# Transposing the normalised rows on TensorE through PSUM in place of eight DMA transposes, with later due times, in a fused attention and FFN layer

## The chip, the cores and the metric

The kernel runs on all 8 cores of one Trainium2 chip, as one program, each core with two of the 16 sequences. The cores exchange nothing. The time is that of the slowest core, in microseconds (us) on the device. A core has TensorE (PE, matmuls; PEld is its weight load), VectorE (DVE), ScalarE (ACT), GpSimd (POOL) and SyncE (SP); the last two issue the DMAs here. Each engine works through its own instructions in order and waits on semaphores.

## What is computed

The input is x [16, 4096, 1024] in f32. One layer, in two halves, with a LayerNorm before and after each half and a residual around it:

```python
def attn(x, Wq, bq, Wk, bk, Wv, bv, Wo, bo):
    q, k, v = (einsum('bsd,kd->bsk', x, W) + b for W, b in ((Wq, bq), (Wk, bk), (Wv, bv)))
    scores = einsum('bqk,bsk->bqs', q, k) / sqrt(1024)
    sign = where(sign(scores) == 0, 1, sign(scores))
    weights = softmax(where(causal, scores * sign, -inf), axis=2)     # scores * sign = abs(scores)
    return einsum('bqv,dv->bqd', einsum('bqs,bsv->bqv', weights, v), Wo) + bo

def ffn(x, kernel, bias, a, b):        # kernel is first rounded to 4-bit steps
    return einsum('bsd,df->bsf', x, int4(kernel)) + bias + (x @ a) @ b     # rank 16

x = x + layernorm(attn(layernorm(x)))
x = x + layernorm(ffn(layernorm(x)))
```

## The kernel before

**Stages.** A prologue quantises and transposes the weights (until about 330 us). Then each of the two sequences goes through phase A (LayerNorm, Q, K and V projections; Q and K go to DRAM scratch, V stays in SBUF) and phase B (attention, output projection, FFN). Phase B lies at about 811 to 2611 us and 3126 to 4941 us of the profiled execution. A barrier stands between the phases. The change touches phase B alone.

**Phase B.** A sequence has 16 strips of 256 queries; strip s has two tiles of 128 rows (qc = 0, 1) and nt = 2s + 2 flash steps, one for each 128 keys up to the diagonal: nt = 2, 4, ... 32. A flash step j issues, in this order: a load of K (L856, on POOL), emit_S (L794: 8 matmuls 128x256 into SBp; ScalarE's Abs to Sa, L802, and Exp to PT, L815; a mask add on VectorE in the last two steps) and emit_PV of step j - 1 (L835: 8 matmuls into OTp, and two of one column for the row sums, L847). SBp, Sa and PT have two slots. PV(j) waits for Exp(j), and S(j) for Abs(j - 2).

**The epilogue, interleaved.** What follows the attention of a strip is not done at once, but as a list of closures with due fractions. `pre` (L575, L583) evicts OTp right at the start of the next strip. `main` (L738 to L748) has both tiles' output projections and all the rest of tile 0; it is popped during the next strip. `spill` (L749 to L757) has the rest of tile 1 and goes one strip later still. In each strip the pending list is the older spill followed by the newer main, and it is popped strictly in order:

```python
while popped < n_pend and int(pend[popped][0] * nt) <= j:
    pend[popped][1]()
    popped += 1
```

So an entry behind a later due time waits for it: the output projections (0.40 and on) come only once store_stage(1) (0.65) has been popped. What is left after the last strip runs without any flash step beside it: the tile spilled by strip 14 and both tiles of strip 15.

**The closures.** outproj_h (L601: 8 matmuls 128x512 into EB; L609 evicts to t1 on ScalarE). lnattn_a (L623 adds bo, then emit_ln into sqb). lnattn_b (L637 adds x into x2, then emit_ln into lnb, bf16). ln2t_dma (L654). xa_stage (L666: lnT against a_bf into EB, L673 copies to xaT). ffn_h (L683, L689, L692 into EB; L697 evicts to t2). lnffn_chain (emit_ln into sqb, L714 adds the residual into xb). store_stage (the store of y on POOL, and on SP the load of x for the tile four further on). EB is a single PSUM bank of 128x512 f32, shared by outproj_h, xa_stage and ffn_h.

**emit_ln** (L174) is one chain over two engines: VectorE's sum (L188) and sum of squares (L191, which writes sqb), L194; ScalarE's L195, L197, L199, L202; VectorE's L204; ScalarE's scaled write (L207). VectorE, ScalarE and POOL instructions are chained in order, so a ScalarE instruction that waits for VectorE holds all later ones, the flash steps' Abs and Exp too.

**ln2t_dma(qc)** issues eight DMA transposes of 128x128 bf16 on SP, from lnb to lnT, each waiting for the LayerNorm's write. xa_stage waits for all eight.

Of the kernel before, what the change touches and what calls it, by code (L numbers as in the profile page):

```python
# [9 lines left out]
AF = mybir.ActivationFunctionType  # L10
# [21 lines left out]
class Builder:  # L32
# [23 lines left out]
    def dma(self, eng, sem, fn, waits=()):  # L56
        sem.n += 16
        self.queue_sems[eng][sem] = True
        self.ops[eng].append(
            (fn, tuple((s.h, int(v)) for s, v in waits if v > 0), ((sem.h, 16),)))  # L60
        return sem.n


def build_nc(debug=False):
# [29 lines left out]
    with ExitStack() as ctx:  # L94
# [59 lines left out]
        E, dma = B.E, B.dma  # L154
# [382 lines left out]
        def phase_b(seq, EB):  # L537
            wl_val = 0
            for rg, src in ((0, wT_scr["wo"]), (1, wfq_h)):
# [14 lines left out]
                "dv_sqb": {0: (DV, 0), 1: (DV, 0)},  # L554
                "ts_done": {0: 0, 1: 0},
                "pe_ffn": {0: 0, 1: 0},
# [12 lines left out]
            def make_epilogue(s):  # L569
# [49 lines left out]
                def lnattn_a(qc):  # L619
                    def f():  # L620
# [5 lines left out]
                                                waits_src=[(DV, dvb)],  # L626
                                                waits_sq=[st["dv_sqb"][qc]])
                        st["dv_t1"][qc] = dv1
# [3 lines left out]
                def lnattn_b(qc):  # L632
                    def f():
# [6 lines left out]
                            waits=[(AC, box["ac_ln1"]), (XS[sl4], st["xs"][t])], incs=[(DV, 1)])[DV]  # L640
                        ac2, dvs2, _ = emit_ln(x2[:], lnb[:, qc * 1024:(qc + 1) * 1024], sq_slot=qc,
                                               waits_src=[(DV, dv_x2)],
                                               waits_sq=[(DV, dv_x2)],
                                               waits_out=[(TS[qc], st["ts_done"][qc])])
                        box["ac_ln2"] = ac2
                        st["dv_sqb"][qc] = (DV, dvs2)
                    return f

                def ln2t_dma(qc):
                    def f():  # L650
                        box = boxes[qc]
                        v = 0
                        for dc in range(8):
                            v = dma("sync", TS[qc], lambda e, dc=dc, qc=qc: e.dma_start_transpose(  # L654
                                out=lnT[:, qc * 1024 + dc * 128:qc * 1024 + (dc + 1) * 128],
                                in_=lnb[:, qc * 1024 + dc * 128:qc * 1024 + (dc + 1) * 128]),
                                waits=[(AC, box["ac_ln2"]), (PE, st["pe_ffn"][qc])])
                        st["ts_done"][qc] = v
                    return f

                def xa_stage(qc):
                    def f():
                        w = [(TS[qc], st["ts_done"][qc]), (AC, st["ac_eb"]),
                             (DV, st["dv_rl"][s])]
# [40 lines left out]
                def lnffn_chain(qc):  # L705
                    def f():
# [4 lines left out]
                                                  waits_src=[(AC, box["fev1"])],  # L711
                                                  waits_sq=[st["dv_sqb"][qc]])
                        st["dv_t2"] = dv1f
# [29 lines left out]
                main.append((0.58, lnattn_b(0)))  # L743
                main.append((0.60, ln2t_dma(0)))
                main.append((0.82, xa_stage(0)))
                main.append((0.86, ffn_h(0, 0)))
                main.append((0.90, ffn_h(0, 1)))
                main.append((0.93, lnffn_chain(0)))  # L748
                spill.append((0.02, lnattn_a(1)))  # L749
                spill.append((0.06, lnattn_b(1)))  # L750
                spill.append((0.08, ln2t_dma(1)))
                spill.append((0.25, xa_stage(1)))
                spill.append((0.25, store_stage(0)))
                spill.append((0.28, ffn_h(1, 0)))
                spill.append((0.32, ffn_h(1, 1)))
                spill.append((0.36, lnffn_chain(1)))
                spill.append((0.65, store_stage(1)))  # L757
                return pre, main, spill
# [203 lines left out]
```

How the kernel before makes its waits and increments, by code:

```python
                def f(e, k=k, bh=BAR.h):  # L165
                    e.drain()
                    e.sem_inc(bh, 1)
                    e.wait_ge(bh, 5 * k)
# [733 lines left out]
            def go(eng):  # L902
                for fn, waits, incs in B.ops[eng_name]:
                    for sh, v in waits:
                        eng.wait_ge(sh, v)
                    inst = fn(eng)
                    if incs:
                        for sh, amt in incs:
                            inst.then_inc(sh, amt)
```

## Time and profile before

| | us |
|---|---|
| median of 5 runs | 5028.55 |
| the 5 runs | 4943.6, 4979.14, 5028.55, 5051.15, 5162.74 |
| the profiled execution | 4942.59 |
| its span on the slowest core (core 6) | 4941.1 |
| span of the 8 cores in it | 4908.7 to 4941.1 |
| TensorE matmuls busy | 2793.3 (57%) |
| ScalarE busy | 1490.3 (30%) |
| VectorE busy | 1286.2 (26%) |
| GpSimd busy | 401.2 (8%) |

The span runs from the first to the last instruction of a core. Busy times come from one profiled execution; matmuls overlap, so a busy TensorE is not one at its peak. The page also lists the chain of work that ended last: followed back from the last instruction, at each step to what released it, with the shares of the span by engine and by line. An engine name with a q (SPq) is its sequencer, issuing DMAs or waiting. The view of waits gives for a line of an engine what it waited for, in total, how often, and the longest. The granted clock is the TensorE clock as a share of 2.4 GHz; 0.50 is its lower level, 1.2 GHz.

### The profile page before, as it was taken

How to read it: one execution, taken by the hardware profiler on the slowest of the kernel's cores; microseconds unless marked ns; L12 is line 12 of the kernel's file. 1: busy time of each engine (PE TensorE's matmuls, PEld its weight loads, DVE VectorE, ACT ScalarE, POOL GpSimd, SP SyncE). 2: the span in 40 equal slices, each digit the busy share in tenths (PEclk: the TensorE clock that was granted, in tenths of full speed). 3: DMA queues.
4: the chain of work that ended last, by engine and by line, in shares of the span. 5: the costliest groups of instructions: out<-in, count | busy, mean ns of one | idle time of the engine just before them, and what ended most of it. 6: DMA issues, size and time to landing. Idle time of an engine off the chain costs nothing.

```text
span 4941.1 us, 56429 instructions; the slowest of 8 cores (4908.7 to 4941.1 us)
## 1 busy us (share of the span) xinstructions
PE 2793.3 (57%) x16447; PEld 1642.6 (33%) x16617; DVE 1286.2 (26%) x1974; ACT 1490.3 (30%) x3073; POOL 401.2 (8%) x725
## 2 busy tenths in 40 slices
PE   1038887344555666666624888534545556666652
PEld 0023333122333444444501333212223334444430
DVE  6732222232222222222222332122222222222222
ACT  0014442222333333333312444122232333333331
POOL 0000000000000111111100000000000011111100
PEclk9999998666777788888856999766777788788876
DMA  2252213111122222333303221311212222233310
GB/s 79 72 185 69 77 60 103 47 56 56 57 74 67 73 76 82 85 86 90 86 15 115 73 73 52 100 53 50 67 57 72 67 79 76 81 84 96 90 58 17
DMA packets 178482, 364.98 MB, mean 74 GB/s; under 512 B 98165, under 2 KB 98293, under 8 KB 176778
## 3 DMA queue, kind: packets, MB, share of 16 engines
q0 software_dynamic: 63680, 220.25, 14.6%
q1 hardware_dynamic: 114506, 141.10, 9.7%
q8 instruction: 147, 2.41, 0.2%
q14 instruction: 149, 1.22, 0.1%
HBM read 266.85 MB, written 77.59 MB: 70 GB/s over the span
## 4 chain that ended last, share of the span: by engine, by line
PE 40%; DVE 20%; ACT 15%; issue 9%; SPq 9%; DMA 6%; ACTq 1%; DVEq 1%; POOLq 0%; POOL 0%
PE SBp L472 8%; SPq L654 8%; PE OTp L835 7%; PE EB L683 6%; PE SBp L794 6%; DVE sqb L191 5%; DVE stats L188 5%; PE EB L601 5%; PE OTp L513 4%; DMA lnT<-lnb 3%; ACT sqb L207 3%; DVE t L329 3%; ACT lnb L207 2%; ACT t L609 2%; DVE x L637 2%
## 5 line engine op out<-in xcount | busy, mean ns | idle before, releaser
L835 PE MATMUL OTp<-PT,V_buf 128*128 128x256 bf16 x4352 | 706.4, 317 | 819.8 <-ACT PT L815 819.8
L835 PEld LDWEIGHTS OTp<-PT,V_buf 128*128 128x128 bf16 x4352 | 475.9, 112 | 970.0 <-issue 862.6
L794 PE MATMUL SBp<-Qs,Ktr 128*128 128x256 bf16 x4352 | 672.7, 308 | 47.1 <-DMA Qs<-q_scr 41.1
L472 PE MATMUL SBp<-lnT,wsl 128*128 128x512 bf16 x2001 | 493.4, 409 | 89.5 <-ACT Qs L479 59.4
L794 PEld LDWEIGHTS SBp<-Qs,Ktr 128*128 128x128 bf16 x4352 | 436.0, 108 | 188.3 <-issue 94.8
L856 POOL DMA_DIRECT2D Ktr<-k_scr x544 | 296.6, 546 | 2367.1 <-PE SBp L794 2287.7
L802 ACT ACTIVATE Sa<-SBp 128x256 f32<-128x256 f32 x544 | 208.5, 383 | 654.6 <-PE SBp L794 632.9
L666 PE MATMUL EB<-lnT,a_bf 128*16 128x128 bf16 x512 | 58.0, 283 | 598.9 <-DMA lnT<-lnb 598.7
L472 PEld LDWEIGHTS SBp<-lnT,wsl 128*128 128x128 bf16 x2048 | 210.8, 104 | 366.7 <-issue 162.7
L683 PE MATMUL EB<-wsl,lnT 128*128 128x512 bf16 x958 | 291.2, 455 | 62.5 <-DVE xaT L673 37.2
L601 PE MATMUL EB<-wsl,OT_sb 128*128 128x512 bf16 x992 | 245.7, 391 | 132.0 <-ACT t L609 127.5
L697 ACT ACTIVATE t<-EB 128x512 f32<-128x512 f32 x128 | 76.4, 597 | 710.8 <-PE EB L692 710.8
L815 ACT ACTIVATE PT<-Sa 128x256 bf16<-128x256 f32 x544 | 226.5, 416 | 169.9 <-ACT Sa L802 96.4
L188 DVE TENSOR_REDUCE stats<-t 128x1 f32<-128x1024 f32 x128 | 156.1, 1220 | 453.7 <-ACT t L697 441.2
L673 DVE CAST xaT<-EB 16x128 bf16<-16x128 f32 x64 | 17.8, 279 | 923.9 <-PE EB L666 923.9
L195 ACT ACTIVATE stats<-stats 128x1 f32<-128x1 f32 x256 | 51.9, 203 | 666.1 <-DVE stats L194 662.7
L666 PEld LDWEIGHTS EB<-lnT,a_bf 128*16 128x16 bf16 x512 | 43.5, 114 | 604.4 <-issue 604.4
L513 PE MATMUL OTp<-wsl,lnT 128*128 128x512 bf16 x999 | 237.9, 380 | 3.0 <-issue 1.9
L527 DVE CAST V_buf<-OTp 128x512 bf16<-128x512 f32 x128 | 88.5, 691 | 561.4 <-PE OTp L519 551.1
L623 DVE TENSOR_TENSOR t<-t,bo_tile 128x1024 f32<-128x1024 f32 x64 | 78.4, 1225 | 422.7 <-ACT t L609 418.9
L601 PEld LDWEIGHTS EB<-wsl,OT_sb 128*128 128x128 bf16 x1024 | 92.8, 99 | 274.0 <-issue 187.3
L207 ACT ACTIVATE sqb<-t,stats 128x1024 f32<-128x1024 f32 x128 | 158.6, 1239 | 63.3 <-DVE stats L204 63.3
(84 smaller groups left out, 2634.4 us busy)
## 6 DMA issues: line engine op xcount, KB each, us to landing
Ktr<-k_scr POOLq DMA_DIRECT2D x544, 256.0 KB, 3.1
xb<-x SPq DMA_DIRECT2D x128, 512.0 KB, 3.8
y<-xb POOLq DMA_DIRECT2D x64, 512.0 KB, 3.1
q_scr<-Qs POOLq DMA_DIRECT2D x32, 512.0 KB, 5.1
k_scr<-Ktr POOLq DMA_DIRECT2D x64, 256.0 KB, 2.9
Qs<-q_scr SPq DMA_DIRECT2D x32, 512.0 KB, 3.6
xb<-fk SPq DMA_DIRECT2D x16, 512.0 KB, 5.4
lnT<-lnb SPq DMA_TRANSPOSE x512, 2.3
```

Source lines behind the costliest of these rows:

```text
L188: E(veng, lambda e, s=src_ap, o=cS1: e.reduce_sum(out=o, in_=s, axis=AX.X), waits=waits_src)
L191: lambda e, s=src_ap, o=sq, a=cS2: e.scalar_tensor_tensor(out=o, in0=s, scalar=1.0, in1=s, op0=ALU.mult, op1=ALU.mult, accum_out=a),
L207: lambda e, s=src_ap, o=out_ap, sc=cR, b=cBn: e.activation(out=o, in_=s, func=AF.Identity, bias=b, scale=sc),
L472: E("tensor", lambda e, wreg=wreg, kc=kc, dc=dc, bk_=bk_: e.matmul(out=SBp[:, bk_ * 512:bk_ * 512 + 512], lhsT=wsl[:, wreg * 8192 + dc * 1 ...
L513: E("tensor", lambda e, sub=sub, h=h, dc=dc, ps=ps: e.matmul(out=ps[:], lhsT=lnT[:, dc * 512 + sub * 128:dc * 512 + (sub + 1) * 128], rhs= ...
L601: E("tensor", lambda e, h=h, vc=vc, qc=qc: e.matmul(out=EB[:], lhsT=OT_sb[:, vc * 256 + qc * 128:vc * 256 + (qc + 1) * 128], rhs=wsl[:, vc ...
L654: v = dma("sync", TS[qc], lambda e, dc=dc, qc=qc: e.dma_start_transpose(out=lnT[:, qc * 1024 + dc * 128:qc * 1024 + (dc + 1) * 128], in_=l ...
L683: E("tensor", lambda e, h=h, dc=dc, qc=qc: e.matmul(out=EB[:], lhsT=lnT[:, qc * 1024 + dc * 128:qc * 1024 + (dc + 1) * 128], rhs=wsl[:, 81 ...
L794: E("tensor", lambda e, j=j, dc=dc, sp=sp, qof=qof: e.matmul(out=SBp[:, sp * 512:sp * 512 + 256], lhsT=Ktr[:, (j % 4) * 1024 + dc * 128:(j ...
L815: r = E("scalar", lambda e, sp=sp: e.activation(out=PT[:, sp * 256:(sp + 1) * 256], in_=Sa[:, sp * 256:(sp + 1) * 256], func=AF.Exp, scale ...
L835: lst=(last and vc % 2 == 1): e.matmul(out=OTp[b_][:, col:col + 256], lhsT=V_buf[:, j * 1024 + vc * 128:j * 1024 + (vc + 1) * 128], rhs=PT ...
L856: st["ks"][j] = dma("gpsimd", KS[j % 4], lambda e, seq=seq, j=j: e.dma_start(out=Ktr[:, (j % 4) * 1024:(j % 4 + 1) * 1024], in_=k_scr[seq, ...
```

## The change

ln2t_dma is replaced by ln2t_pe. The second LayerNorm of a tile writes f32 into sqb[qc] rather than bf16 into lnb. TensorE transposes it in 128x128 blocks against the f32 identity into EB, in two rounds of four, and after each round ScalarE evicts 128x512 from EB to lnT as bf16. Writers of sqb[qc] now also wait for the last transpose that read it. xa_stage waits for the second eviction instead of the DMAs. Most due fractions in main from 0.60 on and nearly all in spill are moved. The DMA transposes, and with them the semaphores' waits, are gone; lnb is no longer used in phase B.

```diff
@@ -552,7 +552,7 @@
                 "ac_eb": 0,
                 "pe_eb_reader": 0,
                 "dv_sqb": {0: (DV, 0), 1: (DV, 0)},
-                "ts_done": {0: 0, 1: 0},
+                "pe_ln2T": {0: 0, 1: 0},
                 "pe_ffn": {0: 0, 1: 0},
                 "dv_xat": 0,
                 "dv_t1": {0: 0, 1: 0},
@@ -624,7 +624,8 @@
                                 waits=[(AC, box["ev1"])], incs=[(DV, 1)])[DV]
                         aca, dvs, dv1 = emit_ln(t1s, sqb[:, qc * 1024:(qc + 1) * 1024], sq_slot=qc,
                                                 waits_src=[(DV, dvb)],
-                                                waits_sq=[st["dv_sqb"][qc]])
+                                                waits_sq=[st["dv_sqb"][qc],
+                                                          (PE, st["pe_ln2T"][qc])])
                         st["dv_t1"][qc] = dv1
                         box["ac_ln1"] = aca
                     return f
@@ -638,29 +639,40 @@
                             out=x2[:], in0=xb[:, sl4 * 1024:(sl4 + 1) * 1024],
                             in1=sqb[:, qc * 1024:(qc + 1) * 1024]),
                             waits=[(AC, box["ac_ln1"]), (XS[sl4], st["xs"][t])], incs=[(DV, 1)])[DV]
-                        ac2, dvs2, _ = emit_ln(x2[:], lnb[:, qc * 1024:(qc + 1) * 1024], sq_slot=qc,
+                        ac2, dvs2, _ = emit_ln(x2[:], sqb[:, qc * 1024:(qc + 1) * 1024], sq_slot=qc,
                                                waits_src=[(DV, dv_x2)],
                                                waits_sq=[(DV, dv_x2)],
-                                               waits_out=[(TS[qc], st["ts_done"][qc])])
+                                               waits_out=[(PE, st["pe_ln2T"][qc])])
                         box["ac_ln2"] = ac2
                         st["dv_sqb"][qc] = (DV, dvs2)
                     return f
 
-                def ln2t_dma(qc):
+                def ln2t_pe(qc):
                     def f():
                         box = boxes[qc]
-                        v = 0
-                        for dc in range(8):
-                            v = dma("sync", TS[qc], lambda e, dc=dc, qc=qc: e.dma_start_transpose(
-                                out=lnT[:, qc * 1024 + dc * 128:qc * 1024 + (dc + 1) * 128],
-                                in_=lnb[:, qc * 1024 + dc * 128:qc * 1024 + (dc + 1) * 128]),
-                                waits=[(AC, box["ac_ln2"]), (PE, st["pe_ffn"][qc])])
-                        st["ts_done"][qc] = v
+                        for rnd in range(2):
+                            wfirst = [(AC, box["ac_ln2"]), (AC, st["ac_eb"])]
+                            for c in range(4):
+                                dc = 4 * rnd + c
+                                E("tensor", lambda e, qc=qc, dc=dc, c=c: e.transpose(
+                                    out=EB[:, c * 128:(c + 1) * 128],
+                                    in_=sqb[:, qc * 1024 + dc * 128:qc * 1024 + (dc + 1) * 128],
+                                    identity=identf[:]),
+                                    waits=wfirst if c == 0 else (), incs=[(PE, 1)] if c == 3 else ())
+                            pe_t = PE.n
+                            r2 = E("scalar", lambda e, qc=qc, rnd=rnd: e.activation(
+                                out=lnT[:, qc * 1024 + rnd * 512:qc * 1024 + (rnd + 1) * 512],
+                                in_=EB[:, 0:512], func=AF.Identity, scale=1.0),
+                                waits=[(PE, pe_t)], incs=[(AC, 1)])
+                            st["ac_eb"] = r2[AC]
+                        st["pe_ln2T"][qc] = PE.n
+                        box["ac_lnT"] = st["ac_eb"]
                     return f
 
                 def xa_stage(qc):
                     def f():
-                        w = [(TS[qc], st["ts_done"][qc]), (AC, st["ac_eb"]),
+                        box = boxes[qc]
+                        w = [(AC, box["ac_lnT"]), (AC, st["ac_eb"]),
                              (DV, st["dv_rl"][s])]
                         for dc in range(8):
                             E("tensor", lambda e, dc=dc, qc=qc: e.matmul(
@@ -709,7 +721,8 @@
                         sl4 = t % 4
                         acf, dvs3, dv1f = emit_ln(t2[:], sqb[:, qc * 1024:(qc + 1) * 1024], sq_slot=qc,
                                                   waits_src=[(AC, box["fev1"])],
-                                                  waits_sq=[st["dv_sqb"][qc]])
+                                                  waits_sq=[st["dv_sqb"][qc],
+                                                            (PE, st["pe_ln2T"][qc])])
                         st["dv_t2"] = dv1f
                         dv_fin = E("vector", lambda e, sl4=sl4, qc=qc: e.tensor_add(
                             out=xb[:, sl4 * 1024:(sl4 + 1) * 1024],
@@ -741,20 +754,20 @@
                 main.append((0.52, outproj_h(1, 1)))
                 main.append((0.54, lnattn_a(0)))
                 main.append((0.58, lnattn_b(0)))
-                main.append((0.60, ln2t_dma(0)))
-                main.append((0.82, xa_stage(0)))
-                main.append((0.86, ffn_h(0, 0)))
+                main.append((0.78, ln2t_pe(0)))
+                main.append((0.84, xa_stage(0)))
+                main.append((0.87, ffn_h(0, 0)))
                 main.append((0.90, ffn_h(0, 1)))
                 main.append((0.93, lnffn_chain(0)))
                 spill.append((0.02, lnattn_a(1)))
                 spill.append((0.06, lnattn_b(1)))
-                spill.append((0.08, ln2t_dma(1)))
-                spill.append((0.25, xa_stage(1)))
-                spill.append((0.25, store_stage(0)))
-                spill.append((0.28, ffn_h(1, 0)))
-                spill.append((0.32, ffn_h(1, 1)))
-                spill.append((0.36, lnffn_chain(1)))
-                spill.append((0.65, store_stage(1)))
+                spill.append((0.30, ln2t_pe(1)))
+                spill.append((0.34, xa_stage(1)))
+                spill.append((0.34, store_stage(0)))
+                spill.append((0.38, ffn_h(1, 0)))
+                spill.append((0.42, ffn_h(1, 1)))
+                spill.append((0.46, lnffn_chain(1)))
+                spill.append((0.70, store_stage(1)))
                 return pre, main, spill
 
             epi_pre = []
```

## Rows read from the trace of the kernel before

**Rows 1.** The page: busy times, and the chain that ended last by engine and line.

```profile
PE 2793.3 (57%) x16447; PEld 1642.6 (33%) x16617; DVE 1286.2 (26%) x1974; ACT 1490.3 (30%) x3073; POOL 401.2 (8%) x725
...
PE 40%; DVE 20%; ACT 15%; issue 9%; SPq 9%; DMA 6%; ACTq 1%; DVEq 1%; POOLq 0%; POOL 0%
PE SBp L472 8%; SPq L654 8%; PE OTp L835 7%; PE EB L683 6%; PE SBp L794 6%; DVE sqb L191 5%; DVE stats L188 5%; PE EB L601 5%; PE OTp L513 4%; DMA lnT<-lnb 3%; ACT sqb L207 3%; DVE t L329 3%; ACT lnb L207 2%; ACT t L609 2%; DVE x L637 2%
```

**Rows 2.** Waits of TensorE, whole span: us in total, times, longest.

```profile
PE OTp L835 <- ACT PT L815: 819.8, 153, 10.5
PE EB L666 <- DMA lnT<-lnb: 598.7, 63, 35.3
...
PE SBp L794 <- DMA Qs<-q_scr: 41.1, 2, 22.0
PE EB L683 <- DVE xaT L673: 37.2, 36, 1.4
```

**Rows 3.** Timeline, 1366 to 1402: start, duration, engine, line, [idle before <-releaser].

```profile
1372.00 1.89 PE L601 MATMUL EB<-wsl,OT_sb 128*128 128x512 bf16 x8 [1.20 <-ACT t L609]
...
1374.60 1.04 PE L835 MATMUL OTp<-PT,V_buf 128*128 128x256 bf16 x8
...
1375.53 1.03 PE L794 MATMUL SBp<-Qs,Ktr 128*128 128x256 bf16 x8
...
1384.28 1.24 ACT L207 ACTIVATE lnb<-x,stats 128x1024 bf16<-128x1024 f32 x1 [0.48 <-DVE stats L204]
...
1385.65 10.03 SPq L654 DMA_TRANSPOSE lnT<-lnb  x8
...
1386.70 0.38 ACT L802 ACTIVATE Sa<-SBp 128x256 f32<-128x256 f32 x1
1386.75 1.87 PE L835 MATMUL OTp<-PT,V_buf 128*128 128x256 bf16 x8 [10.19 <-ACT PT L815]
1387.29 0.42 ACT L815 ACTIVATE PT<-Sa 128x256 bf16<-128x256 f32 x1 [0.20 <-ACT Sa L802]
...
1397.22 1.01 PE L666 MATMUL EB<-lnT,a_bf 128*16 128x128 bf16 x8 [8.57 <-DMA lnT<-lnb]
1398.16 1.89 PE L794 MATMUL SBp<-Qs,Ktr 128*128 128x256 bf16 x8
```

**Rows 4.** Waits of TensorE at L666, in 811:1100, 2484:2611 and 3150:3420.

```profile
PE EB L666 <- DMA lnT<-lnb: 98.2, 5, 23.9
...
PE EB L666 <- DMA lnT<-lnb: 86.0, 3, 35.3
...
PE EB L666 <- DMA lnT<-lnb: 98.0, 5, 23.5
```

**Rows 5.** Timeline and single lines: f32 weight loads, bf16 transposes, the f32 transpose.

```profile
5.69 3.48 PEld L233 LDWEIGHTS LBp<-onesrowf,rowstage 1*128 1x128 f32 x16 [5.69 <-issue]
...
256.42 1.14 PE L361 MATMUL TRs<-ident,Qs 128*128 128x128 bf16 x8 [1.22 <-DVE wsl L374]
...
339.14 1.15 PE L434 MATMUL TRA<-ident,lnb 128*128 128x128 bf16 x8 [21.04 <-ACT lnb L207]
...
L295 PE MATMUL LBp<-identf,gq x1: 371/371/371, 46.2 to 46.2; 128*1 128x128 f32 x1
```

**Rows 6.** Groups by form: count | busy us, mean ns of one | idle before.

```profile
L683 PE MATMUL EB<-wsl,lnT 128*128 128x512 bf16 x958 | 291.2, 455 | 62.5 <-DVE xaT L673 37.2 <-ACT t L697 21.0 <-issue 2.6
...
L513 PE MATMUL OTp<-wsl,lnT 128*128 128x512 bf16 x999 | 237.9, 380 | 3.0 <-issue 1.9
...
L207 ACT ACTIVATE sqb<-t,stats 128x1024 f32<-128x1024 f32 x128 | 158.6, 1239 | 63.3 <-DVE stats L204 63.3
...
L583 ACT ACTIVATE OT_sb<-OTp 128x512 bf16<-128x512 f32 x128 | 76.4, 597 | 54.0 <-PE LBp L847 44.2
```

**Rows 7.** Stretches: engines' busy us, granted clock, DMA share, GB/s.

```profile
1360.00:1376.00 16.00, 12.04 (x82) 7.17 (x81) 3.83 (x5) 5.14 (x11) 1.09 (x2) 1.00 0.29 99
1386.00:1397.00 11.00, 1.90 (x10) 1.35 (x10) 0.00 (x0) 1.22 (x3) 0.00 (x0) 0.50 0.14 26
```

## Prediction

> **What bounds the kernel now.** I read the page first. TensorE's matmuls are busy for 57% of the span, ScalarE for 30%, VectorE for 26% [rows 1]. So no engine is full, and the time is in waits. The chain that ended last says which: beside TensorE's own lines it holds 9% of SyncE's queue and 6% of DMA, with L654 alone 8% and the landing of lnT<-lnb another 3% [rows 1]. In microseconds that is about 0.12 x 4941 = 590. TensorE is the one in-order stream through which every stage of phase B passes, so its waits are read next. Two lines hold nearly all: 819.8 us for ScalarE's exponentials (L835 behind L815) and 598.7 us, 63 times, for the transposed lnT (L666) [rows 2]. The chain and the wait name the same 590 to 600 us.
>
> The timeline around one tile, in a strip with nt = 12, shows how both arise [rows 3]. When the four out-projections are done, two LayerNorms run one after the other on VectorE and ScalarE, of which [rows 3] shows the last write. ScalarE takes its work in order, so the exponential of the next flash step stands behind them: TensorE gets through S, PV, S and then idles 10.19 us (first kind of wait). ScalarE writes lnb at 1384.28 to 1385.52. Then SyncE issues eight DMA transposes, 10.03 us, the last lands and L666 starts at 1397.22: 11.7 us after lnb was complete. TensorE had only one PV (with its row sums) to put under that and idles 8.57 us (second kind).
>
> **How much of the 598.7 us is the transposes.** The change can only remove what lies behind the end of lnb, at most 11.7 us per tile. Where a wait is longer, TensorE reached L666 while the LayerNorms still ran. Those are the first tiles of each sequence (stretches 811:1100 and 3150:3420, 98.2 and 98.0 us in 5 waits each, of which one is 8.6 us and four are 21.5 to 23.9) and its last three tiles, behind the last flash step (2484:2611, 86.0 us in 3 waits; 4786:4941 reads the same 86.0) [rows 4]. Capped, they are 2 x (4 x 11.7 + 8.6 + 3 x 11.7) = 181 us. The other 47 waits count whole: 598.7 - 98.2 - 98.0 - 2 x 86.0 = 230 us. Sum: 411 us. The remaining 188 us are LayerNorm time and will reappear as a wait of the new transposes.
>
> **What the change adds on TensorE.** For each of the 64 tiles: eight transposes of 128x128 f32, in two rounds of four because EB is one bank, and two ScalarE evictions of 128x512, f32 to bf16.
>
> The trace has no 128x128 f32 stationary. Nearest rows [rows 5]: eight bf16 transposes take 1.15 us at L434; the one f32 transpose (L295, one column stationary) is a single pass of 371 ns; f32 weight loads of 128 columns come 16 in 3.48 us, 0.22 us each. Lower bound 1.15 us as in bf16; upper bound, with load and pass not overlapping, 8 x (0.22 + 0.37) = 4.7 us. I take 8 x 0.22 plus one pass of 0.37 at the end of each round, 2.5 us, since everywhere else in the trace loads run under the matmuls.
>
> Between the rounds TensorE waits for the eviction. The same pattern, matmul, eviction of EB, next matmul, is L601 behind L609: 1.20 us [rows 3]. ScalarE is free by then: after S(j) its Abs and Exp take 0.38 + 0.20 + 0.42 us, under PV. An eviction of the new form (L583) takes 0.60 us [rows 6], 0.09 less than L609's, which is inside that 1.20; I keep 1.2. The second eviction is hidden by the next S and PV (1.03 + 1.04 us) unless the transposes and xa_stage fall in the same step j. Working out int(fraction x nt) with the list's in-order popping gives that for nt = 4 and 8 in main, nt = 8, 10, 14, 20 in spill, and the last three tiles: 9 per sequence, 18 x 1.2 = 22 us. Both evictions together are 77 us more of ScalarE, which has the room: a warm flash step is 2.07 us of TensorE and 1.0 us of ScalarE.
>
> Cost so far: 64 x (2.5 + 1.2) + 22 = 259 us.
>
> **What the change moves.** The due fractions. store_stage(1) goes from 0.65 to 0.70, and since the list is popped in order it holds back the out-projections and both LayerNorms of the other tile. ln2t_pe comes only 0.08 of nt later. Today L666 stands two or more steps behind for nt >= 10, so TensorE can put S, PV, S under the LayerNorms. With the change TensorE meets the transposes first: in the same step as the LayerNorms for nt = 6 and 10 (nothing fits under them: S and PV are lost for 6, S, PV, S for 10), and one step later for nt = 12, 14, 16, 20 (one S lost each). That is 2 + 3 + 4 = 9 units of 1.03 (full clock) to 1.89 us, 18 in both sequences: 25 us. For the spill tile (transposes at 0.30) nothing is lost. By the same arithmetic xa_stage and ffn_h(.,0) share a step in 36 cases today, which is the count of L683's waits for xaT in [rows 2], and in 30 with the change: 6 waits of 37.2 / 36 = 1.03 us less, 6 us. On SyncE's queue only loads of x and Q stand behind the removed transposes, and TensorE never waits for a load in mid-sequence [rows 2], so their earlier issue gives nothing. The later stores (0.34 and 0.70) delay loads wanted two strips later. ScalarE writes f32 to sqb in 1239 ns [rows 6], bf16 to lnb in 1.24 us [rows 3]. The new waits on sqb are for transposes that ended long before, queued on the same engines in order: nothing.
>
> **The clock.** In the wait of [rows 3] the granted clock is 0.50, the level of 1.2 GHz; while the out-projections run it is 1.00, 2.4 GHz [rows 7]. The S behind the wait then takes 1.89 us instead of 1.03 [rows 3]. The FFN matmuls, which follow L666, pay most: L683 averages 455 ns and L513, the same form in dense work, 380 [rows 6]. 1024 x 0.075 = 77 us. So between 0 and 77 us come back with the idle gap; I take half, 40, as the gap is not removed but cut into pieces.
> By the Trainium skill (TensorE: Matmul & The Clock Gate, "Part 4: PE-mode transpose") a transpose does not count as TensorE being busy, so the new stretch would act like idleness and nothing would come back. The granted clock of a stretch of transposes between flash steps stands in no row here, so no run so far decides it; rival C below is this mechanism, worked out from rows.
>
> **The sum.** Saved: 411 + 6 + 40 = 457. Added: 259 + 25 = 284. Net 173 us off the profiled execution, which took 4942.6 us: 4769 us, a factor of 0.965. The five runs have a median of 5028.55, 1.7% above that execution, so on their footing 5028.55 x 0.965 = 4852 us.
> All at the cheap end: 64 x (1.15 + 1.1) + 20 + 18 = 182 added (1.1 for the shorter eviction, covers warm), 411 + 6 + 77 = 494 saved, 312 net, factor 0.937, 4711 us. The dear end are the rivals.
>
> **The rivals.** About 2% is what a measurement of this kernel can tell from no change.
> A, the forecast: TensorE idle is exchanged for 3.7 us of transposing per tile. Chance 0.67 of more than 2% faster. For it: the critical chain itself holds the transposes' 11 to 12%, and the waits on both sides of them are on the same in-order engine, so they don't overlap with another bound.
> B, the f32 loads don't run under the passes: 4.7 us per tile. 64 x 5.9 + 47 = 425 added, 457 saved: 32 us net, 4996 us. For it: 0.22 us per f32 load where a bf16 transpose takes 1.15 / 8 = 0.14 us with its load [rows 5]. Against it: bf16 loads run under the pass before everywhere. Chance 0.14, same.
> C, the clock: the gap pieces and the transposes leave TensorE at 1.2 GHz each time. Then the 40 us don't come back and each tile pays a slow S and PV more, 2 x 0.85 = 1.7 us, 109 us in all: 173 - 149 = 24 us net, 5004 us. For it: at L361, where TensorE does nothing but transposes between waits of about 1.2 us, eight take 1.14 us, no faster than the first eight of L434 behind a wait of 21 us [rows 5]. Against it: the flash steps between the pieces are dense. Chance 0.09, same.
> D, the other side: f32 passes are doubled. Every f32 matmul of the prologue is recorded as two (L233: 16 for the 8 that the loop issues) [rows 5]. Without overlap that is 8 x 2 x 0.59 = 9.4 us and 1.2 per tile, 678 + 47 = 725 added against 457: 268 us slower, 5300 us. Break-even is (457 - 47) / 64 = 6.4 us per tile, and more than 2% slower begins at 8.0. Against it: the f32 transpose L295 is recorded once. Chance 0.06.
> E, TensorE, let go sooner, waits longer for ScalarE, and half of the 411 us come back at L835: 173 - 206 = 33 us lost, 5062 us. Against it: those waits are LayerNorm latencies that start with TensorE's own out-projections and FFN matmuls, so they move along with it. Chance 0.04, same.
>
> Faster 0.67, same 0.27 (B, C and E), slower 0.06. The range is 4710 to 5000: from the cheap end to just past B, leaving out D and E, and C by 4 us.
>
> **What will show it.** L654 gone from SyncE and from the chain. No wait at L666 longer than about 1.3 us. A new wait of the first transpose for ScalarE's LayerNorm output, some 190 us plus lost cover, largest in the strips with small nt and the last three tiles. 512 f32 transposes in groups of four, a group about 1.2 us, and 64 waits of about 1.2 us before the second group. L835's wait for L815 near 800 us. L683's mean below 455 ns. The prediction is wrong if a group of four takes over 2.3 us (B), if L683's mean rises above 455 ns (C), if there are 1024 transpose records (D), or if L835's wait grows by what L666's lost.

## The result, and the profile after

| | before | after |
|---|---|---|
| median, us | 4961.75 (10 runs) | 4659.6 (6 runs) |
| profiled execution's span, us | 4941.1 | 4643.0 |
| ratio to before | | 0.940, 95% interval 0.936 to 0.944 |

The change makes the kernel 6.0% faster. The forecast had the direction and 3.5%; the time lies below its range, which began at 4710. Some executions of this 8-core program run 1.5 to 7% longer, with a lower granted clock on one die or both, whatever the kernel; the five under the forecast held several of them, and the ratios here compare undisturbed ones. Ten runs of the kernel before have a median of 4961.75, not 5028.55.

The page after: busy times, and the chain that ended last by engine.

```profile
PE 2829.6 (61%) x17129; PEld 1687.2 (36%) x17129; DVE 1286.4 (28%) x1974; ACT 1567.4 (34%) x3201; POOL 402.9 (9%) x725
...
PE 48%; DVE 21%; ACT 17%; issue 8%; DMA 3%; ACTq 1%; DVEq 1%; POOLq 0%; SPq 0%; POOL 0%
```

SyncE's 9% and half of the DMA's 6% are gone from the chain [rows 1], ScalarE has 77 us more, as worked out, and TensorE 36. The waits of TensorE after (us in total, times, longest). L848 is L835 of before, L807 is L794, L695 is L683, L678 is L666; L657 are the new transposes, L663 their eviction:

```profile
PE OTp L848 <- ACT PT L828: 740.3, 148, 10.9
PE EB L657 <- ACT sqb L207: 298.9, 24, 23.6
...
PE EB L657 <- ACT lnT L663: 58.6, 64, 1.3
...
PE EB L695 <- DVE xaT L685: 21.2, 30, 0.7
PE EB L678 <- ACT lnT L663: 20.5, 18, 1.4
```

The 598.7 us of [rows 2] have become 298.9 us for the LayerNorms, 58.6 us between the two rounds (64 times) and 20.5 us for the second eviction (18 times, as counted). L695 waits for xaT 30 times, as counted. The wait for the exponentials fell by 80 us, which the forecast had not said.

Groups by form after (count | busy us, mean ns | idle before):

```profile
L848 PE MATMUL OTp<-PT,V_buf 128*128 128x256 bf16 x4352 | 687.8, 311 | 740.3 <-ACT PT L828 740.3
L807 PE MATMUL SBp<-Qs,Ktr 128*128 128x256 bf16 x4352 | 661.2, 305 | 42.4 <-DMA Qs<-q_scr 40.2 <-ACT OT_sb L583 2.0 <-DMA Ktr<-k_scr 0.2
...
L695 PE MATMUL EB<-wsl,lnT 128*128 128x512 bf16 x1024 | 265.9, 406 | 44.4 <-ACT t L709 23.2 <-DVE xaT L685 21.2
...
L657 PE MATMUL EB<-identf,sqb 128*128 128x128 f32 x512 | 115.6, 368 | 357.5 <-ACT sqb L207 298.9 <-ACT lnT L663 58.6
```

The 512 transposes take 115.6 us, 1.8 us per tile. The FFN matmuls average 406 ns instead of 455 [rows 6]. The timeline of the tile that answers to [rows 3] (the same strip, nt = 12):

```profile
1313.14 1.89 PE L601 MATMUL EB<-wsl,OT_sb 128*128 128x512 bf16 x8 [1.20 <-ACT t L609]
1314.87 1.04 PE L807 MATMUL SBp<-Qs,Ktr 128*128 128x256 bf16 x8
1315.74 1.04 PE L848 MATMUL OTp<-PT,V_buf 128*128 128x256 bf16 x8
...
1326.91 1.08 PE L657 MATMUL EB<-identf,sqb 128*128 128x128 f32 x4 [10.11 <-ACT sqb L207]
...
1328.15 0.60 ACT L663 ACTIVATE lnT<-EB 128x512 bf16<-128x512 f32 x1 [0.40 <-PE EB L657]
...
1328.89 1.09 PE L657 MATMUL EB<-identf,sqb 128*128 128x128 f32 x4 [0.89 <-ACT lnT L663]
1329.77 1.92 PE L807 MATMUL SBp<-Qs,Ktr 128*128 128x256 bf16 x8
1331.48 1.91 PE L848 MATMUL OTp<-PT,V_buf 128*128 128x256 bf16 x8
...
1333.35 0.75 PE L678 MATMUL EB<-lnT,a_bf 128*16 128x128 bf16 x8
```

Only S and PV stand under the LayerNorms, one unit less than before, as forecast. From the end of the out-projections (1313.14 + 1.89 = 1315.0) to xa_stage at 1333.35 it is 18.3 us; in [rows 3] it was 23.3 us, from 1373.9 to 1397.2. A round is 1.08 us even at the lower clock (granted 0.50 from 1327 to 1333), and the gap between rounds 0.89 us, not 1.20.

### The profile page after: what moved, and what is told of

The parts are those of the page before. It is cut to its first block, busy times and chain, and to the rows that moved or that the text cites. A ratio compares the mean times of both kernels' runs of the same rounds, so it can differ in the third digit from the quotient of the medians.

```text
span 4643.0 us, 56877 instructions; the slowest of 8 cores (4612.5 to 4643.0 us)
## 1 busy us (share of the span) xinstructions
PE 2829.6 (61%) x17129; PEld 1687.2 (36%) x17129; DVE 1286.4 (28%) x1974; ACT 1567.4 (34%) x3201; POOL 402.9 (9%) x725
## 4 chain that ended last, share of the span: by engine, by line
PE 48%; DVE 21%; ACT 17%; issue 8%; DMA 3%; ACTq 1%; DVEq 1%; POOLq 0%; SPq 0%; POOL 0%
PE OTp L848 10%; PE SBp L472 9%; PE SBp L807 7%; PE EB L695 6%; DVE sqb L191 5%; DVE stats L188 5%; ACT sqb L207 5%; PE EB L601 5%; PE OTp L513 5%; DVE t L329 3%; PE EB L657 2%; ACT t L609 2%; DVE x L638 2%; ACT stats L199 2%; ACT stats L197 2%
## 5 line engine op out<-in xcount | busy, mean ns | idle before, releaser
L848 PE MATMUL OTp<-PT,V_buf 128*128 128x256 bf16 x4352 | 687.8, 311 | 740.3 <-ACT PT L828 740.3
L848 PEld LDWEIGHTS OTp<-PT,V_buf 128*128 128x128 bf16 x4352 | 468.5, 110 | 883.2 <-issue 782.5
L807 PE MATMUL SBp<-Qs,Ktr 128*128 128x256 bf16 x4352 | 661.2, 305 | 42.4 <-DMA Qs<-q_scr 40.2
L807 PEld LDWEIGHTS SBp<-Qs,Ktr 128*128 128x128 bf16 x4352 | 435.1, 108 | 173.7 <-issue 83.8
L657 PE MATMUL EB<-identf,sqb 128*128 128x128 f32 x512 | 115.6, 368 | 357.5 <-ACT sqb L207 298.9
L601 PE MATMUL EB<-wsl,OT_sb 128*128 128x512 bf16 x1024 | 253.5, 392 | 124.3 <-ACT t L609 122.1
L695 PE MATMUL EB<-wsl,lnT 128*128 128x512 bf16 x1024 | 265.9, 406 | 44.4 <-ACT t L709 23.2
L657 PEld LDWEIGHTS EB<-identf,sqb 128*128 128x128 f32 x512 | 76.2, 186 | 382.2 <-issue 382.2
L601 PEld LDWEIGHTS EB<-wsl,OT_sb 128*128 128x128 bf16 x1024 | 93.2, 99 | 269.5 <-issue 183.8
L609 ACT ACTIVATE t<-EB,rl 128x512 f32<-128x512 f32 x128 | 88.0, 687 | 300.1 <-PE EB L601 292.7
```

Source lines behind the costliest of these rows:

```text
L601: E("tensor", lambda e, h=h, vc=vc, qc=qc: e.matmul(out=EB[:], lhsT=OT_sb[:, vc * 256 + qc * 128:vc * 256 + (qc + 1) * 128], rhs=wsl[:, vc ...
L657: E("tensor", lambda e, qc=qc, dc=dc, c=c: e.transpose(out=EB[:, c * 128:(c + 1) * 128], in_=sqb[:, qc * 1024 + dc * 128:qc * 1024 + (dc + ...
L695: E("tensor", lambda e, h=h, dc=dc, qc=qc: e.matmul(out=EB[:], lhsT=lnT[:, qc * 1024 + dc * 128:qc * 1024 + (dc + 1) * 128], rhs=wsl[:, 81 ...
L807: E("tensor", lambda e, j=j, dc=dc, sp=sp, qof=qof: e.matmul(out=SBp[:, sp * 512:sp * 512 + 256], lhsT=Ktr[:, (j % 4) * 1024 + dc * 128:(j ...
L848: lst=(last and vc % 2 == 1): e.matmul(out=OTp[b_][:, col:col + 256], lhsT=V_buf[:, j * 1024 + vc * 128:j * 1024 + (vc + 1) * 128], rhs=PT ...
```

## The experiments

The theory that the forecast left me with: its mechanism is right, its terms are too dear on the cost side and too low for the clock. Rivals: the new due times are what pays; or the wait removed is worth more than its 411 us, because TensorE is slow behind it. The first four kernels take the change apart.

**frac**, the kernel before with the new due fractions alone:

```diff
-main.append((0.82, xa_stage(0)))
+main.append((0.84, xa_stage(0)))
 ...
-spill.append((0.25, xa_stage(1)))
+spill.append((0.34, xa_stage(1)))
-spill.append((0.65, store_stage(1)))
+spill.append((0.70, store_stage(1)))
```

> The kernel before with only the due fractions of the change; the eight DMA transposes stay. If the fractions are a small part of the gain (my prediction, which gave them +25 - 6 us): the waits of the spilled tiles at L666 shrink because xa_stage stands at 0.34 instead of 0.25, by some 45 us per sequence, the others grow a little; 4942 to about 4860 us, ratio 0.983. If the change's gain comes mostly from the new due times: near 4700, ratio 0.95. If they only cost: 4960 or more.

Measured: ratio 0.9985 (0.9969 to 1.0001), no change. My 0.983 was a miss. Waits of core 6 (granted clock 0.807, as before), to be compared with [rows 2]:

```profile
PE OTp L835 <- ACT PT L815: 834.9, 157, 10.9
PE EB L666 <- DMA lnT<-lnb: 581.8, 55, 35.3
```

Eight of the 63 waits at L666 are gone, but the sum fell by only 17 us, and the exponentials' wait rose by 15. I had counted the tiles that gain and passed over those that now have less between the LayerNorms and xa_stage. The gaps in front of xa_stage, read from both traces for core 6, say so: in the spilled tiles they fell from 288 to 210 us, in the others they rose from 311 to 372. So the due times alone pay nothing.

**pe_oldfrac**, the changed kernel with the old due fractions:

```diff
-main.append((0.78, ln2t_pe(0)))
+main.append((0.60, ln2t_pe(0)))
 ...
-spill.append((0.30, ln2t_pe(1)))
+spill.append((0.08, ln2t_pe(1)))
 ...
```

> The changed kernel with the old due fractions, so that the transposes on TensorE are popped together with, or right behind, the LayerNorms. Theory that the later due times matter because TensorE has nothing to put under the LayerNorms otherwise: three units of a flash step (about 1.2 us each) lost per tile in some 26 of 32 tiles per sequence, about +150 us on the changed kernel's 4643: 4790, ratio to before 0.970. Theory that due times don't matter: 4643, ratio 0.940.

Measured: ratio 0.9523 (0.9492 to 0.9554): 0.0121 above the changed kernel, 60 us. Its waits (core 6; the granted clock of this profile is 0.809, that of the executions behind the ratio 0.828, so the sums are rough):

```profile
PE EB L657 <- ACT sqb L207: 809.3, 64, 23.6
PE OTp L848 <- ACT PT L828: 314.4, 89, 7.7
```

The two together are 1124 us against 1039 after: some 85 us of cover lost, where I had expected 150. So transposes on TensorE need the later due times, and these are worth 60 us there. Now every tile waits, 64 times: TensorE stands at the transposes instead of at an exponential.

**none_old**, the kernel before without any transposing:

```diff
-for dc in range(8):
-    v = dma("sync", TS[qc], ... dma_start_transpose(...))
-st["ts_done"][qc] = v
+st["ts_done"][qc] = 0
 ...
-w = [(TS[qc], st["ts_done"][qc]), ...]
+w = [(AC, boxes[qc]["ac_ln2"]), ...]
```

> The kernel before with its eight DMA transposes per tile left out; lnT keeps stale rows, so the FFN half computes with wrong inputs, and xa_stage waits for the LayerNorm's write instead. It is the whole worth of the transposes' wait. Clock theory (the idle gap also slows what follows): 411 us of waiting and some 90 us of slow matmuls go, 4942 to about 4441, ratio 0.90. Without the clock: 4531, ratio 0.917. If the wait moves on to the exponentials (rival E): above 4700, ratio over 0.95.

Measured: ratio 0.9055 (0.9027 to 0.9082), span 4474.1 against 4941.1: 467 us. Its waits and groups:

```profile
PE OTp L829 <- ACT PT L809: 828.8, 155, 10.5
PE EB L660 <- ACT lnb L207: 192.0, 14, 23.7
...
L829 PE MATMUL OTp<-PT,V_buf 128*128 128x256 bf16 x4352 | 683.5, 310 | 828.8 <-ACT PT L809 828.8
...
L677 PE MATMUL EB<-wsl,lnT 128*128 128x512 bf16 x958 | 264.3, 422 | 59.3 <-DVE xaT L667 34.8 <-ACT t L691 21.3 <-issue 0.9
```

Here the cap of the forecast is measured: 192.0 us remain, in 14 waits, where it said 188 in 14 (four and three per sequence). 598.7 - 192.0 = 407 us were transposing. The exponentials' wait stayed (828.8 against 819.8), so rival E falls. The other 60 us are not this wait: PV's mean fell from 317 to 310 ns and the FFN's from 455 to 422.

**fill**, the kernel before with TensorE kept working in that wait:

```diff
 def xa_stage(qc):
     def f():
+        for i_ in range(FILL[(s, qc)]):
+            E("tensor", lambda e: e.matmul(out=EB[:], lhsT=wsl[:, 0:128],
+              rhs=wsl[:, 0:512], start=True, stop=True), waits=... if i_ == 0 else ())
```

FILL is the measured wait of the tile, less 0.8 us, over 0.216 us where it is under 5 us, and 8 + (wait - 4.4) / 0.216 where it is longer: 2188 matmuls in all.

> The kernel before with idle matmuls (128x512, into EB, overwritten by xa_stage) in front of xa_stage, their number chosen per strip to fill most of the measured wait for the DMA transposes without overrunning it. The wait stays as long, but TensorE works in it. Clock theory: what follows runs at the full clock, L683's mean goes from 455 to about 400 ns and 60 to 90 us are saved, ratio 0.985. If the clock is not worth anything here, or the fill overruns: ratio 1.00 or above.

Measured: ratio 0.9867 (0.9845 to 0.989), 66 us faster with 2188 matmuls more. The mean granted clock went from 0.81 to 0.87. Its wait at xa_stage and its FFN group:

```profile
PE EB L673 <- DMA lnT<-lnb: 107.9, 55, 4.3
...
L690 PE MATMUL EB<-wsl,lnT 128*128 128x512 bf16 x966 | 264.9, 419 | 53.3 <-DVE xaT L680 27.6 <-ACT t L704 21.5 <-issue 0.9
```

The transposes still take as long: from the LayerNorm's write to xa_stage it is 792 us in total over the 64 tiles, 788 before. Only the idleness is gone. So 60 to 66 us are the price of TensorE standing idle there, by two different routes.

The second four price the new work and look for a better kernel.

**double**, the changed kernel with every group of four issued twice:

```diff
-for c in range(4):
+for c in (0, 1, 2, 3, 0, 1, 2, 3):
 ...
```

The semaphore is incremented by the last of the eight.

> The changed kernel with each group of four transposes issued twice in a row (the second writes the same values). It measures what a transpose costs by itself. From the changed kernel's trace a group adds about 0.86 us to TensorE's time: 128 groups, 110 us, 4643 to about 4750, ratio to before 0.961. My prediction's 2.5 us per tile would make it +160 us, 0.972. If transposes did not count as work for the clock and slowed what follows (rival C): more than 0.975 and L695's mean well above 406 ns.

Measured: ratio 0.9601 (0.9525 to 0.9678), span 4730.7 against 4643.0: 88 us for 512 more. The transposes' group:

```profile
L658 PE MATMUL EB<-identf,sqb 128*128 128x128 f32 x1024 | 203.3, 364 | 356.6 <-ACT sqb L207 299.4 <-ACT lnT L666 57.2
```

203.3 - 115.6 = 87.7 us busy and 87.7 us of span: an f32 transpose costs about 0.17 us, 1.4 us per tile, and nearly all of it is on the path. That the two agree to 0.1 us is luck: the ratios put the difference at 0.020, 98 us, with an interval of some 40 us to either side, and the medians of the two dies at 91 and 73 us. The FFN's mean did not rise (403 ns), which speaks against rival C.

**none_new**, no transposing with the new due fractions (the edits of none_old and frac together):

> The kernel before with the transposes left out (stale lnT, wrong FFN inputs) and the new due fractions: the same work as the changed kernel without any transposing. If the new fractions matter only as cover for the transposes: as with the old fractions, ratio 0.905, and the changed kernel's whole price of transposing is about 173 us above it. If they gain by themselves: 0.89 or less.

Measured: ratio 0.9069 (0.9053 to 0.9085), as with the old ones. The fractions are worth something only as cover. The changed kernel's price of transposing is 0.9402 - 0.9069 = 0.033, 165 us.

**bf16one**, one round in bf16:

```diff
+EBb = EB.bitcast(BF16)
 ...
-emit_ln(x2[:], sqb[...], ...)
+emit_ln(x2[:], lnb[...], ...)
 ...
-for rnd in range(2): (four f32 transposes into EB, evict 128x512)
+for dc in range(8):
+    e.transpose(out=EBb[:, dc * 128:(dc + 1) * 128], in_=lnb[...], identity=ident[:])
+e.activation(out=lnT[...], in_=EBb[:, 0:1024], func=AF.Identity, scale=1.0)
```

> The changed kernel, but the LayerNorm writes bf16 into lnb, the eight transposes are bf16 and fill EB's bank once (seen as 1024 bf16), and one eviction of 128x1024 takes them out. The wait between the groups (0.92 us each, 59 us) goes, transposes cost about 1.0 us per tile instead of 1.7 (-45 us), the longer eviction shows in the 18 tiles where xa_stage follows at once (+8 us): 4643 to about 4546, ratio 0.920. If f32 is not dearer than bf16: 0.930.

Measured: ratio 0.9195 (0.914 to 0.9251), as expected. The transposes' group:

```profile
L656 PE MATMUL EB<-ident,lnb 128*128 128x128 bf16 x512 | 55.1, 273 | 299.4 <-ACT lnb L207 299.4
```

No wait between rounds, 55.1 us instead of 115.6, and the LayerNorm wait is untouched (299.4).

**spread**, bf16one with the work of a strip spread out:

```diff
-main.append((0.40, outproj_h(0, 0)))     ... 0.44, 0.48, 0.52
+main.append((0.44, outproj_h(0, 0)))     ... 0.47, 0.50, 0.53
-... lnattn_a(0) 0.54, lnattn_b(0) 0.58, ln2t_pe(0) 0.78
+... lnattn_a(0) 0.55, lnattn_b(0) 0.64, ln2t_pe(0) 0.73
-spill: lnattn_a(1) 0.02, lnattn_b(1) 0.06, ln2t_pe(1) 0.30, ... store_stage(1) 0.70
+spill: lnattn_a(1) 0.00, lnattn_b(1) 0.09, ln2t_pe(1) 0.18, ... store_stage(1) 0.42
```

> As bf16one, with due fractions spread out: store_stage(1) at 0.42 so that the out-projections come at 0.44 to 0.53, the two LayerNorms at 0.55 and 0.64 and the transposes at 0.73, each with flash steps between (spill: 0.00, 0.09, 0.18). Theory: each LayerNorm in ScalarE's queue blocks the exponentials until it ends, whatever stands behind it, and TensorE can put at most S, PV, S under each block; two blocks with three units each hide more than one block of both. About 3 units of 1.2 us more per tile where strips are long enough, some 90 us: ratio 0.902. If the blocks hide nothing more, or each pays a slow clock of its own: 0.92 or above.

Measured: ratio 0.8993 (0.8972 to 0.9015). The size is as expected, but not made as expected. Its waits:

```profile
PE OTp L847 <- ACT PT L827: 505.3, 152, 8.6
PE EB L656 <- ACT lnb L207: 289.9, 30, 23.7
...
PE SBp L806 <- DMA Ktr<-k_scr: 172.5, 28, 13.1
```

The exponentials' wait fell by 230 us against bf16one (735.4), far more than the 90 I had put on it, and a wait that was at most 5 us in every earlier kernel took 172.5 of them back: K loads. They stand on GpSimd's queue behind the store of y, and the store, now close behind lnffn_chain, waits there for VectorE: 896.3 us in all, 564.7 in the changed kernel.

The last three kernels settle what these left open.

**spread2**, the same with the store taken out of the way:

```diff
-spill.append((0.42, store_stage(1)))
+spill.append((0.62, store_stage(1)))
 ...
-pend = list(spill_next) + list(e_main)
+pend = sorted(list(spill_next) + list(e_main), key=lambda p_: p_[0])
```

> The run with spread due times, where 172.5 us of waits for K loads had appeared: each store of y right behind lnffn_chain waits on GpSimd's queue for VectorE, and the K loads stand behind it. Here store_stage(1) goes to 0.62, and the pending list is sorted by due time so that it no longer holds back the out-projections. If that queue is the cause: the K waits fall below 30 us, TensorE's waits for the exponentials rise by some of it, and 4443 becomes about 4330, ratio 0.876. If the K waits have another cause: they stay, ratio 0.90.

Measured: ratio 0.8665 (0.8646 to 0.8684), 13.4% faster than before and the fastest of all. Its waits, and the S group with what is left of the K wait:

```profile
PE OTp L847 <- ACT PT L827: 543.8, 163, 8.6
PE EB L656 <- ACT lnb L207: 290.1, 30, 23.7
...
L806 PE MATMUL SBp<-Qs,Ktr 128*128 128x256 bf16 x4352 | 644.1, 299 | 42.9 <-DMA Qs<-q_scr 39.9 <-DMA Ktr<-k_scr 2.1 <-ACT OT_sb L584 0.9
```

The K wait is 2.1 us, so the queue was the cause; the later store and the sorted list came in together and were not tried apart. 38 us came back at the exponentials.

**mm2**, two rounds as in the change, but bf16 and by ordinary matmuls against the identity:

```diff
-emit_ln(x2[:], sqb[...], ...)
+emit_ln(x2[:], lnb[...], ...)
 ...
-e.transpose(out=EB[...], in_=sqb[...], identity=identf[:])
+e.matmul(out=EB[...], lhsT=lnb[...], rhs=ident[:], start=True, stop=True)
```

> The changed kernel with the LayerNorm written as bf16 into lnb and the blocks turned by ordinary bf16 matmuls against the identity, in the same two rounds of four and with the same two evictions. It takes only f32 out. If f32 costs what the trace says (1.7 against about 0.8 us per tile in the one-round run): 60 us less than the changed kernel, ratio 0.929, and the second round with its longer wait is the other half of the one-round run's gain. If the rounds are what cost: near 0.940.

Measured: ratio 0.9389 (0.9373 to 0.9406), not to be told from the change's 0.9402 (0.936 to 0.944). A miss. Its groups:

```profile
L848 PE MATMUL OTp<-PT,V_buf 128*128 128x256 bf16 x4352 | 701.5, 315 | 741.1 <-ACT PT L828 741.1
...
L657 PE MATMUL EB<-ident,lnb 128*128 128x128 bf16 x512 | 65.2, 270 | 361.7 <-ACT lnb L207 298.9 <-ACT lnT L663 62.9
```

The turning itself got 50 us cheaper (65.2 against 115.6), but PV 14 us dearer (701.5 against 687.8), S 5 (666.2 against 661.2) and the wait between the rounds 4. That is 23 of the 50; the spans are 12 apart, so another 15 are not found in these rows. In bf16one, with one round, PV went the other way, to 678.4. Shorter pieces with the same gap between them may have left more slow matmuls behind; whether the gap, the kind of instruction or neither did it was not taken apart and stays open.

**fill_tr**, the fill with transposes in place of matmuls:

```diff
-for i_ in range(FILL[(s, qc)]):   matmul 128x512
+for i_ in range(4 * FILL[(s, qc)]):
+    e.transpose(out=EBb[:, (i_ % 8) * 128:...], in_=wsl[:, (i_ % 8) * 128:...], identity=ident[:])
```

> The kernel before, its waits for the DMA transposes filled as in the run with idle matmuls, but with bf16 128x128 transposes, four in place of each matmul of 512 columns (the same columns), into EB and overwritten by xa_stage. If a transpose keeps TensorE's clock up like a matmul: the same 1.3% as the run with matmuls, ratio 0.987, and the granted clock near 0.87. If transposes leave the clock as idleness does: no gain, ratio 1.00, or above where the slower transposes overrun the wait; granted clock near 0.81.

Measured: ratio 0.9955 (0.9937 to 0.9973), granted clock 0.867. Half right: the clock is that of the fill with matmuls, the time is not. Three stretches in which TensorE does nothing but transposes (engines' busy us, granted clock, DMA share, GB/s). The first two are one fill, behind a wait of 8.20 us and one PV at 0.50; the third lies before the last xa_stage of the first sequence. Below them, 10 us of the same wait in the kernel before:

```profile
913.30:916.30 3.00, 3.00 (x32) 3.00 (x31) 0.28 (x2) 1.70 (x5) 0.00 (x0) 0.50 0.27 104
917.00:935.00 18.00, 18.00 (x326) 18.00 (x324) 3.99 (x6) 3.04 (x7) 0.00 (x0) 1.00 0.08 16
...
2557.00:2590.00 33.00, 33.00 (x595) 33.00 (x593) 11.48 (x18) 6.71 (x15) 0.53 (x1) 1.00 0.09 26
```

```profile
2582.00:2592.00 10.00, 0.00 (x0) 0.00 (x0) 0.00 (x0) 0.29 (x1) 0.00 (x0) 0.50 0.12 23
```

Transposes alone hold 2.4 GHz, and between the first two stretches the clock rose to it while only transposes ran. The gain was lost elsewhere, and not by overrunning: TensorE still waited for the DMA in 59 of the 64 tiles, for longer than in fill (107.9).

```profile
PE EB L675 <- DMA lnT<-lnb: 134.5, 59, 4.0
```

The DMA transposes themselves had become slower. SyncE needed 10.88 us on average to issue the eight of a tile, against 10.34 in fill and 10.29 before, and from the LayerNorm's write to xa_stage it was 831 us in total, against 792 in fill: 39 of the 44 us by which the ratios differ. For the last tile of the first sequence, fill_tr and then fill:

```profile
2579.33 10.57 SPq L657 DMA_TRANSPOSE lnT<-lnb  x8
```

```profile
2538.11 10.02 SPq L656 DMA_TRANSPOSE lnT<-lnb  x8
```

Why they became slower stays open. One thing that differs between the two pages is the DMA queue named q8 instruction, 3.52 MB against 2.69.

## Why the prediction was right or wrong

The direction, the place and the counts of tiles held. The sum did not: 173 us forecast, 298 measured (4941.1 - 4643.0). The steps that failed are two terms of it: what comes back through the clock was put at 40 us, half of a bound that counted the FFN's matmuls alone, and the eight transposes at 160 us. Together they make 100 of the 125 us by the rows. Term by term, measured from the rows above:

| term | forecast | measured |
|---|---|---|
| wait removed | 411 | 407 (598.7 - 192.0) |
| xaT waits saved | 6 | 16 (37.2 - 21.2) |
| back through the clock | 40 (0 to 77) | 96 by the rows, 60 to 66 by none_old and fill |
| eight transposes | 160 (2.5 each tile) | 116 (1.8) |
| wait between the rounds | 77 (1.2) | 59 (0.92) |
| second eviction | 22 | 20.5 |
| lost cover | 25 | 27 |
| net | 173 | 297 |

Lost cover is the change of both LayerNorm waits together: 740.3 + 298.9 - 819.8 - 192.0 = 27 (18 with none_old's own 828.8). The xaT waits are 30 as counted, but each took 0.71 us in place of 1.03. The clock's 96 are the busy times of S (11.5), PV (18.6), xa (58.0 - 46.4), the FFN's 1024 matmuls (49 ns each, 50) and the two bias rows (4). The lines for it, before and then after:

```profile
L835 PE MATMUL OTp<-PT,V_buf 128*128 128x256 bf16 x4352 | 706.4, 317 | 819.8 <-ACT PT L815 819.8
L794 PE MATMUL SBp<-Qs,Ktr 128*128 128x256 bf16 x4352 | 672.7, 308 | 47.1 <-DMA Qs<-q_scr 41.1 <-ACT OT_sb L583 6.0
...
L666 PE MATMUL EB<-lnT,a_bf 128*16 128x128 bf16 x512 | 58.0, 283 | 598.9 <-DMA lnT<-lnb 598.7 <-issue 0.2
```

```profile
L678 PE MATMUL EB<-lnT,a_bf 128*16 128x128 bf16 x512 | 46.4, 244 | 20.5 <-ACT lnT L663 20.5
```

The 96 is a high reading: added up in the same way, none_old's rows give 84, where its span leaves 60. That the terms close to 1 us is therefore in part luck. With 60 to 66 for the clock the transposes are the larger error, and some 30 us of the measured gain are not assigned.

**What held.** The critical chain and TensorE's wait named the same time, and only the part behind the LayerNorm's write went. none_old leaves 192 us where 188 was worked out. The counts from int(fraction x nt), 18 second evictions and 30 waits for xaT, are exact, and the cover lost is within 2 to 7 us. Counting the order by hand paid; only frac, where I looked at one kind of tile and not at the other, missed.

**The clock, mis-sized.** The step said between 0 and 77 us, from the FFN's matmuls alone, and took half "as the gap is not removed but cut into pieces". The bound was too narrow: PV, S and xa run slow behind the gap too, 42 us by the rows, and they had been left out although [rows 3] showed S at 1.89 instead of 1.03. And half was too little: the pieces are 0.9 us long with work between them, and the FFN recovered 50 of its 77 us. fill shows the clock by itself at 66 us, without any wait removed.

**The transposes, mis-sized.** 2.5 us per tile came from 0.22 us for each f32 load and a whole pass at the end of each round. The trace has 1.8, and double prices the marginal one at about 0.17 us. A round is 0.90 us on average (115.6 / 128) where the forecast had 1.25. The loads of that row came 0.22 us apart; the four of a round of L657 take 0.71 us, 0.18 each, even at the lower clock. The 1.2 us between the rounds came from L601 behind L609, although the step itself saw that the new eviction is 0.09 us shorter. The two steps around it shrank too, from TensorE's end to ScalarE's start from 0.26 to 0.16 us and from ScalarE's end to TensorE's start from 0.24 to 0.14, and 0.89 to 0.92 us remained; why is not shown.

**The rivals.** B (loads not under the passes, 4.7 us per tile) and D (doubled passes) fall by the 512 records in 115.6 us. E falls by none_old. C falls twice: the FFN's mean went down, not up, and fill_tr shows the granted clock at 1.00 through 33 us of transposes alone, and rising from 0.50 to 1.00 while they ran. The Trainium skill (TensorE: Matmul & The Clock Gate, "Part 4: PE-mode transpose") says that transposes do not count as TensorE being busy for its clock. The measurement differs and decides: on this chip, in this kernel, they did.

**The wait for the exponentials.** I expected it near 800 us; it is 740.3, while the LayerNorm wait is 298.9 instead of about 213. They are one wait in two places: TensorE stands still until the LayerNorms end, at the next exponential or at the transposes, whichever it meets first. pe_oldfrac has 426 us less of the one (740.3 to 314.4) and 510 more of the other (298.9 to 809.3). Only their sum says what an edit did.

**The footing.** The factor 0.9402 lies just inside the forecast's cheap end of 0.937; the time does not, as that end was set on a median of 5028.55. On the median of ten runs the same factor gives 4961.75 x 0.937 = 4649 us, below the 4659.6 measured. So the mis-sized terms moved the estimate, and the footing put the time outside the range.

## What to carry to other kernels

A wait of an in-order engine costs its length and the slow matmuls behind it: here 407 us of waiting were worth 467, and the second part can be measured by filling the wait with idle work. When several long chains share ScalarE with the steps that TensorE lives on, spread them and put a few steps between each: that alone, with the K loads freed, took 5.3% of the time before more (0.9195 to 0.8665). Before moving a store on a queue, ask what stands behind it there: one store, due too early, brought 172.5 us of waits for loads.

## What the runs showed of the hardware

- Transposes held the granted clock at 1.00 for 33 us with nothing else on TensorE, and it also rose from 0.50 to 1.00 during a run of them (fill_tr). 604 of them, bf16 128x128, took 33.88 us, 0.056 us each (core 6 of fill_tr):

```profile
2541.97 33.88 PE L667 MATMUL EB<-ident,wsl 128*128 128x128 bf16 x604 [0.95 <-ACT t L706]
```

- An f32 128x128 transpose costs about 0.17 us in this kernel (88 us of span for 512 on the slowest cores, 73 to 98 by other counts). Its weight load takes 137 to 231 ns, bf16 95 to 152:

```profile
L657 PEld LDWEIGHTS EB<-identf,sqb x512: 137/183/231, 869.7 to 4610.0; 128*128 128x128 f32 x171
...
L657 PEld LDWEIGHTS EB<-ident,lnb x512: 95/103/152, 876.2 to 4596.4; 128*128 128x128 bf16 x171
```

The first line is of the changed kernel, the second of mm2.

- One PSUM bank of 128x512 f32, seen as 128x1024 bf16, takes eight bf16 transposes and one eviction in place of two rounds; together with bf16 for f32 this was worth 0.021 of the time before (0.9402 to 0.9195).
- Eight DMA transposes, with TensorE idle or on matmuls, took 10.3 us to issue on average; with TensorE on transposes all the while 10.9 (64 tiles each). The cause is not shown.
